# Layer norm of the query moved from GpSimd to VectorE, with all four engines' instructions reordered

## What is computed

```
x = x + xattn(ctx, layernorm(x), key_bias, seq_len)     # softmax over 128 keys, 16 heads
x = x + down(silu(gate(layernorm(x))) * up(layernorm(x)))  # inner width 512
# every linear: activation rounded to 127 / max|row|, weight to {-1, 0, 1} * mean|w|
```

## Time and profile before

| | us |
|---|---|
| median of 3 runs | 181.34 (181.11 to 182.14) |
| the profiled execution | 181.3, of which the span from first to last instruction is 179.2 |
| busy: DVE, POOL, PE, ACT | 148.7, 142.1, 141.4, 130.6 |

### The profile page before, as it was taken

The page is one execution under the profiler, slowest core; times in us unless marked ns, Lnnn a source line. Parts: engine busy times, 40 slices in busy tenths (PEclk is TensorE's granted clock), DMA queues, the critical chain, the costliest instruction groups (busy, mean ns, idle before and its releaser), DMA issues. The chain is left out here.

```text
span 179.2 us, 6662 instructions
## 1 busy us (share of the span) xinstructions
PE 141.4 (79%) x2211; PEld 89.2 (50%) x2211; DVE 148.7 (83%) x519; ACT 130.6 (73%) x197; POOL 142.1 (79%) x274
## 2 busy tenths in 40 slices
PE   0015999999998998999999995667777888988562
PEld 0013776666666665666666663112345454555441
DVE  0446767889979898988988888899999999999972
ACT  0005788988978897988888887856785989987541
POOL 7387978889867997888899999998999846774430
PEclk9999999999999999999999999555597999999985
DMA  1999993000000000000000000000001111111222
GB/s 41 308 286 299 287 294 80 4 0 5 5 4 0 5 4 2 4 4 4 0 7 4 4 2 4 2 0 2 0 15 32 46 29 46 49 44 29 60 77 59
DMA packets 16353, 9.61 MB, mean 54 GB/s; under 512 B 1088, under 2 KB 15424, under 8 KB 16320
## 3 DMA queue, kind: packets, MB, share of 16 engines
q1 hardware_dynamic: 15600, 8.39, 17.6%
q10 hardware_dynamic: 720, 0.80, 1.3%
HBM read 7.09 MB, written 2.10 MB: 51 GB/s over the span
## 5 line engine op out<-in xcount | busy, mean ns | idle before, releaser
L517 ACT ACTIVATE probs<-scores,bias_all 128x1024 f32<-128x1024 f32 x64 | 68.5, 1112 | 2.9 <-PE scores L633 2.4
L650 PE MATMUL outs<-probs,v_ones 128*32 128x128 f32 x1024 | 41.9, 283 | 0.1
L618 PE MATMUL turned<-ident_h,k_parts 128*128 128x128 f16 x128 | 19.3, 230 | 15.9 <-DVE q_parts L821 13.6
L650 PEld LDWEIGHTS outs<-probs,v_ones 128*32 128x32 f32 x1024 | 24.7, 111 | 9.0 <-issue 5.8
L633 PE MATMUL scores<-stacks 32*128 32x128 f16 x512 | 26.1, 224 | 1.4 <-DVE stacks L829 1.3
L445 POOL TENSOR_SCALAR hr<-h,h_fac 128x512 f32<-128x512 f32 x32 | 21.9, 692 | 6.5 <-DVE h_fac L910 6.2
L553 ACT ACTIVATE hqT<-turned 128x512 bf16<-128x512 int16 x32 | 19.1, 596 | 8.4 <-PE outs L719 7.7
L829 DVE COPY stacks<-turned 128x512 f32<-128x512 f32 x32 | 21.4, 670 | 4.2 <-PE turned L620 4.1
L546 ACT ACTIVATE silu_g<-scores,gate_s 128x512 f32<-128x512 f32 x32 | 22.0, 688 | 1.6 <-PE scores L691 0.6
L618 PEld LDWEIGHTS turned<-ident_h,k_parts 128*128 128x128 f16 x128 | 12.6, 102 | 19.9 <-issue 16.0
L898 DVE TENSOR_REDUCE h_peak<-h 128x1 f32<-128x512 f32 x32 | 21.5, 672 | 0.0
(11 more groups left out here) (81 smaller groups left out, 293.7 us busy)
## 6 DMA issues: line engine op xcount, KB each, us to landing
result<-x_all SPq DMA_DIRECT2D x32, 64.0 KB, 1.5
k_all<-in_ctx SPq DMA_DIRECT2D x1, 1024.0 KB, 10.8
v_all<-in_ctx SPq DMA_DIRECT2D x1, 1024.0 KB, 10.9
x_all<-in_x SPq DMA_DIRECT2D x1, 512.0 KB, 7.7
k_all<-in_ctx SPq DMA_DIRECT2D x1, 512.0 KB, 7.0
v_all<-in_ctx SPq DMA_DIRECT2D x1, 512.0 KB, 7.1
x_all<-in_x SPq DMA_DIRECT2D x2, 128.0 KB, 5.5
k_all<-in_ctx SPq DMA_DIRECT2D x2, 128.0 KB, 6.6
```

The costliest lines, as they stand in the source:

```text
L517: act.activation(probs[:, p, 8 * a:8 * a + 8, :].rearrange("p h q -> p (h q)"), scores[:, HALF * a:HALF * (a + 1)], ACT.Exp, bias=bias_all ...
L618: pe.transpose(turned_h[:, g * 128:(g + 1) * 128], k_parts[:, p4, heads, :, :].rearrange("p h c d -> p (h c d)"), ident_h[:, :])
L650: last = pe.matmul(sums_ps(p)[32 * g:32 * (g + 1), 128 * r:128 * (r + 1)], pair[:, 32 * i:32 * (i + 1)], probs[:, p, GROUPS * (2 * r + i) ...
```

## The change

- `q_norm` leaves POOL and is made by DVE with one `scalar_tensor_tensor`, `(x - mean1) * rstd1`, with `rstd1` broadcast along the features as its second tensor. `minus1_of` and its semaphore go.
- The lists of all four engines get new offsets and a new order. On DVE `q_norm` stands at -4, `q_low` at -6, `stack_out` at -7, `denom`, `attn` and `x1` at -11 (were -8, -8 and -9).
- The total of the weights moves from step 18 into `sum_a` of batch 3; clips, scales and casts of the weights move to earlier steps.
- OUT_AFTER_X goes from 14 to 12, X_BEFORE_OUT from 12 to 10. The wait of `x1_of` for `q_done` goes: both are on DVE now.

```diff
-SUM_STEP = 7
-W_TOTAL = 18
-OUT_AFTER_X = 14
-X_BEFORE_OUT = 12
+W_BATCH = 3
+OUT_AFTER_X = 12
+X_BEFORE_OUT = 10
...
# GpSimd
-            def q_norm(t, k):
-                arrived(pool, x_in, t, k)
-                pool.wait_ge(minus1_done, t.count(k))
-                pool.wait_ge(rstd1_done, t.count(k))
...
-                pool.tensor_scalar(q_f[:, t.side(k, 4), :], x_all[:, t.at(k), :].rearrange("p b d -> p (b d)"),
-                                   minus1[:, t.slot(k)], rstd1[:, t.slot(k)], ALU.add, ALU.mult).then_inc(q_done, 1)
...
-                if s == 21:
+                if s == 18:
                     w_clip(0)
-                if s == 35:
                     w_scale(0)
-                if s == 37:
+                if s == 25:
                     w_clip(1)
+                if s == 26:
                     w_clip(2)
+                if s == 30:
                     w_scale(1)
+                if s == 32:
                     w_scale(2)
-                t.run_pair(k_high, 0)
-                t.run_pair(v_beside_ones, -4)
-                t.run_pair(vare1_of, 0)
-                t.run(q_norm, -2)
-                t.run_pair(rstd1_of, 0)
-                t.run_pair(k_low, -1)
-                t.run_quad(vare2_of, -25)
+                t.run_pair(k_high, -7)
+                t.run_pair(rstd1_of, -5)
                 t.run_quad(rstd2_of, -26)
-                t.run(q_high, -2)
+                t.run(q_high, -8)
+                t.run_pair(k_low, -7)
+                t.run_pair(v_beside_ones, -10)
+                t.run_quad(vare2_of, -21)
+                t.run_pair(vare1_of, -3)
+                t.run(h_round, -56)
                 t.run(y_of, -29)
-                t.run(x_round, -39)
-                t.run(h_round, -52)
+                t.run(x_round, -46)
# ScalarE
+                if s == 23:
+                    w_cast(0)
                 if s == 37:
-                    w_cast(0)
-                if s == 38:
                     w_cast(1)
...
-                t.run(weigh_a, -5)
-                t.run(weigh_b, -5)
                 t.run(sums_of, -6)
-                t.run(xqT_out, -42)
-                t.run(silu_of, -43)
-                t.run(hqT_out, -52)
+                t.run(weigh_a, -4)
+                t.run(weigh_b, -4)
+                t.run(xqT_out, -46)
+                t.run(hqT_out, -56)
+                t.run(silu_of, -46)
# TensorE
+                if t.numbers is None and t.value(k) == W_BATCH:
+                    w_total_of(t, k)
...
+                t.run(score_b, -7)
                 t.run(stack_turn, -5)
-                t.run(score_b, -6)
-                t.run(sum_a, -7)
-                t.run(sums_turn, -8)
-                t.run(sum_b, -7)
-                t.run(score_a, -5)
+                t.run(sum_a, -8)
+                t.run(sums_turn, -9)
+                t.run(sum_b, -8)
+                t.run(score_a, -6)
+                t.run(project_gate, -45)
                 t.run(down, -55)
-                t.run(project_up, -44)
-                t.run(xq_turn, -42)
-                t.run(project_gate, -43)
-                t.run(hq_turn, -52)
+                t.run(xq_turn, -44)
+                t.run(hq_turn, -53)
+                t.run(project_up, -45)
# VectorE
+            def q_norm(t, k):
                 dve.wait_ge(mean1_done, t.count(k))
+                dve.wait_ge(rstd1_done, t.count(k))
...
+                dve.scalar_tensor_tensor(q_f[:, t.side(k, 4), :], x_all[:, t.at(k), :].rearrange("p b d -> p (b d)"),
+                                         mean1[:, t.at(k), 0:1].rearrange("p b o -> p (b o)"),
+                                         rstd1[:, t.at(k)].broadcast_to([128, D]), ALU.subtract, ALU.mult).then_inc(q_done, 1)
...
-                if s == 7:
+                if s == 8:
                     w_sum_of(0)
-                if s == 8:
                     w_sum_of(1)
-                if s == 15:
+                if s == 10:
                     w_sum_of(2)
-                if s == W_TOTAL:
+                if s == 13:
                     w_mean_of()
...
-                t.run(x1_of, -9)
                 t.run(stats1_of, 0)
-                t.run_pair(minus1_of, -1)
-                t.run(stats2_of, -9)
-                t.run(mean2_of, -11)
-                t.run(stack_out, -5)
+                t.run(q_low, -6)
                 t.run(mean1_of, 0)
-                t.run(denom_of, -8)
-                t.run_quad(minus2_of, -12)
-                t.run(q_low, -4)
-                t.run(attn_of, -8)
-                t.run(h_peak_of, -47)
-                t.run_quad(h_factor, -48)
-                t.run_quad(x_factor, -33)
-                t.run(h_of, -46)
-                t.run_quad(out_scale, -52)
-                t.run(finish, -56)
-                t.run_quad(gate_scale, -34)
-                t.run_quad(x_unit_of, -32)
-                t.run_quad(floor_of, -34)
-                t.run_quad(h_unit_of, -47)
-                t.run(y_peak_of, -31)
+                t.run(q_norm, -4)
+                t.run(denom_of, -11)
+                t.run(stats2_of, -12)
+                t.run(attn_of, -11)
+                t.run_quad(minus2_of, -18)
+                t.run(mean2_of, -14)
+                t.run(stack_out, -7)
+                t.run(x1_of, -11)
+                t.run_quad(h_factor, -49)
+                t.run(h_of, -47)
+                t.run_quad(x_factor, -30)
+                t.run_quad(out_scale, -52)
+                t.run_quad(h_unit_of, -48)
+                t.run_quad(floor_of, -33)
+                t.run(finish, -56)
+                t.run_quad(gate_scale, -30)
+                t.run_quad(x_unit_of, -29)
+                t.run(y_peak_of, -28)
+                t.run(h_peak_of, -47)
```

More of the change, by code:

```diff
@@ L174, in attention_feed_forward @@
         mean1 = sb("mean1", [128, B, 2])
-        minus1 = sb("minus1", [128, B])
         vare1 = sb("vare1", [128, B])
@@ L256, in attention_feed_forward @@
         k_hi, k_lo, v_set = sem("k_hi"), sem("k_lo"), sem("v_set")
-        stats1_done, mean1_done, minus1_done = sem("stats1_done"), sem("mean1_done"), sem("minus1_done")
+        stats1_done, mean1_done = sem("stats1_done"), sem("mean1_done")
         vare1_done, rstd1_done = sem("vare1_done"), sem("rstd1_done")
@@ L392, in rstd1_of @@
                 pool.tensor_tensor(rstd1[:, t.slot(k, 2)], vare1[:, t.slot(k, 2)], half_power[:, 0:n], ALU.pow).then_inc(rstd1_done, n)
-            def q_norm(t, k):
-                arrived(pool, x_in, t, k)
-                pool.wait_ge(minus1_done, t.count(k))
-                pool.wait_ge(rstd1_done, t.count(k))
-                if t.has(k - 4):
-                    pool.wait_ge(q_hi, t.count(k - 4))
-                    pool.wait_ge(q_lo, t.count(k - 4))
-                pool.tensor_scalar(q_f[:, t.side(k, 4), :], x_all[:, t.at(k), :].rearrange("p b d -> p (b d)"),
-                                   minus1[:, t.slot(k)], rstd1[:, t.slot(k)], ALU.add, ALU.mult).then_inc(q_done, 1)
             def q_high(t, k):
@@ L597, in w_total_of @@
                 pe.wait_ge(w_summed, 3)
-                pe.wait_ge(attn_done, t.count(k - 2))
                 pe.matmul(outs[t.side(k)][:, 0:3], ones[:, :], w_sum[:, :], start=True, stop=True).then_inc(w_total, 1)
@@ L790, in w_mean_of @@
                 dve.wait_ge(w_total, 1)
[L791 removed]
+                dve.tensor_scalar(w_mean[:, :], outs[W_BATCH % 2][:, 0:3], 1.0 / (INNER * D), QUANT_EPS, ALU.mult, ALU.max).then_inc(w_meaned, 1)
                 dve.wait_ge(w_meaned, 1)
@@ L807, in mean1_of @@
                 dve.bn_aggr(mean1[:, t.slot(k), :].rearrange("p b c -> p (b c)"), stats1[:, t.slot(k), :].rearrange("p b c -> p (b c)")).then_inc(mean1_done, 1)
-            def minus1_of(t, k):
-                n = t.group(2)
+            def q_norm(t, k):
                 dve.wait_ge(mean1_done, t.count(k))
-                dve.tensor_scalar(minus1[:, t.slot(k, 2)], mean1[:, t.slot(k, 2), 0:1].rearrange("p b o -> p (b o)"), -1.0, None,
-                                  ALU.mult).then_inc(minus1_done, n)
+                dve.wait_ge(rstd1_done, t.count(k))
+                if t.has(k - 4):
+                    dve.wait_ge(q_hi, t.count(k - 4))
+                    dve.wait_ge(q_lo, t.count(k - 4))
+                dve.scalar_tensor_tensor(q_f[:, t.side(k, 4), :], x_all[:, t.at(k), :].rearrange("p b d -> p (b d)"),
+                                         mean1[:, t.at(k), 0:1].rearrange("p b o -> p (b o)"),
+                                         rstd1[:, t.at(k)].broadcast_to([128, D]), ALU.subtract, ALU.mult).then_inc(q_done, 1)
             def q_low(t, k):
@@ L843, in x1_of @@
                 xb = x_all[:, t.at(k), :].rearrange("p b (g r i) -> p (b r) g i", g=GROUPS, r=2)
-                if not t.shift:
-                    dve.wait_ge(q_done, t.count(k))
                 dve.tensor_tensor(xb, xb, attn[:, t.side(k), :].rearrange("p (r g i) -> p r g i", r=2, g=GROUPS), ALU.add).then_inc(x1_done, 1)
```

(6 more changed lines are left out.)

3 lines of the change are left out of this document (removed).

## The result

The changed kernel takes 176.78 us (median of 4, 176.29 to 176.97) beside 181.23 us of the kernel before, run with it: a ratio of 0.9744, interval 0.9701 to 0.9786. The forecast was 178.3 us, "faster" with 0.67. The profiled execution took 176.67 us, with a span of 174.5.

A forecast was written before the change was run, and what follows sets the result against it. Attention was taken as held by order and waiting, feed-forward by DVE work. From 181.3 us, +0.3 - 1.9 - 0.45 - 0.3 - 1.1 + 0.5 = -2.95 gave 178.3 us, range 175.8 to 183.0.

The forecast's parts named there:

- the rival that TensorE sets the pace: Attention: PE fully sets 2.73 us per batch, -3.8 us instead of -1.9, total 176.4 us; chance 0.13.
- the slower rival: Attention: DVE becomes the bound at 3.0 us per batch through waits behind POOL, +3.7 us, total 183.9; chance 0.15.
- The loop: Attention: POOL's `k_high` waits for PE's key turn, which needs DVE's q_low after POOL's work; new order removes the stalls.
- The pace: Attention: spacing of ScalarE's copies of the sums, once per batch, from 2.867 to 2.80 us over 28 spacings, -1.9 us.
- 2.73 us remains their floor: Attention, PE and ACT: stack_turn moves, work is unchanged, so the best spacing of 2.73 us per batch stays the limit.
- the weights' stop: Attention: PE waits for the mean of the weights, a short stall that stays in the new order; counted in 2.80 us.
- The lock: Attention: DVE instructions with two SBUF inputs contend with POOL instructions reading SBUF, the later blocked; 0.34 us per batch allowed.
- A random moment: Attention: if DVE's instructions met POOL's at random, each would wait 0.20 us, three per batch, giving 3.0 us per batch.
- phases that miss each other: Attention: DVE and POOL mostly fall into phases without meeting, read from x1's mean of 0.300 with POOL busy 89%.
- The start: Start to second copy of the sums: first exponential 1.5 to 2 us later, mostly won back; net +0.3 (0 to +2).
- Change of stage: Attention to feed-forward: one xqT copy fewer before the table load, -0.45, and lighter POOL for the peaks of y, -0.3.
- Feed-forward and tail: Feed-forward stage and tail: -1.1 for peaks and small scales leaving the stage, +0.5 for the silu chain and later h_factor.

The follow-up runs named there:

- the four corners: Old or new order, each with `q_norm` on POOL or DVE, against the kernel before: old 1 and 0.9939, new 0.9998 and 0.9744.
- The run with the swap: Changed kernel with stack_turn put back ahead of score_b in TensorE's list: 178.30 us, ratio 0.9793, pace 2.740.
- The replaced k_low: Changed kernel with POOL's k_low subtraction replaced by a memset of zeros, leaving out the keys' fp16 remainder: 172.53 us, pace 2.591.
- The kernel with the early pair: Changed kernel with q and k work of batches 0 and 1 ahead of the stages of later loads: 173.95 us, ratio 0.9614.
- the old lists: Changed kernel with the feed-forward halves of all four engine lists and both window constants as before, attention still new: 177.35 us, ratio 0.9800.
- the runs with equal clocks: Changed kernel with stack_turn ahead of score_b (178.30 us) or batches 0 and 1 early (173.95 us), tails compared at TensorE clocks 0.90 and 0.78.

## Why the prediction was right, and where its terms were not

The sign, the mechanism and the range held; two terms were wrong by about 2.7 us each, in opposite directions, and the total is closer than its parts. That they cancel is luck. 176.78 us lies inside the stated range of 175.8 to 183.0, but under the forecast's own band of 177 to 179.7, which had 0.50; it is next to the 176.4 of the rival that TensorE sets the pace, which had 0.13. DVE became the bound of attention, as the slower rival had it, and the kernel was faster all the same.

**The loop.** "Its stalls go. What is late next is DVE." Shown: the wait before `k_high` falls from 11.2 to 1.2 us, and the four corners show that it takes the order and the lighter POOL together. POOL's saved 16.9 us alone would have bought 0.6%.

**The pace: -1.9 predicted, -4.65 measured.** The step that failed is "2.73 us remains their floor", and the 2.80 built on it. Two sizes were off. First, DVE's need: the prediction put 2.74 us per batch, the trace has 74.14 / 28 = 2.65. It is lower although x1's wait was underrated, partly because the stretch holds only 24 of 28 `q_norm` and 20 of the first statistics: the deeper offsets have moved the others into the start. Second, the floor: it lay in the place of one stage in TensorE's list, and the diff shows that this place changes. The run with the swap parts the two: with the old place 28 x (2.740 - 2.867) = -3.56 us, the move itself a further -1.1. So the larger share of the miss, 28 x 0.06 = 1.7 us, is the "friction" and the weights' stop that made 2.80 out of 2.74: the floor of 2.73 was met almost exactly as long as the stage kept its place. The sentence on PE named the move and priced it at nothing; the best spacing of a trace is a floor for that order of instructions only. "Work is unchanged" was true of the instructions and not of the time they take: the scores need 7.3 us less when their halves are neighbours. The forecast's nearness of DVE to TensorE was right all the same: 2.65 stands beside 2.58.

**The lock.** The prediction allowed 0.34 us per batch for waiting behind POOL. By the means over the whole span it is 0.50: `q_low` 523 ns where 360 is free, `q_norm` 449 for 313, x1 487 for 290. That lies between the forecast and the 0.60 of the slower rival, which had a chance of 0.15. Held against its own marks: `q_low` (under 550, right), `q_norm` (just in its band), x1 (over 450, one half of the slower rival's mark; the other half, means above 0.6, didn't come). The replaced k_low alone accounts for 0.25 us a batch. In each encounter with k_low shown the DVE instruction ends 0.08 to 0.16 us after it, a `q_norm` that is over in 0.31 when free after 1.31. The Trainium skill's rule ("SBUF — State Buffer", Who interferes with whom: the later of the two waits until the other is through) agrees with these rows in that DVE's instruction ends right behind POOL's. It isn't seen in them who was first: the two at 13.07 and 13.08 start 0.01 and 0.02 us ahead of POOL's and wait all the same. How often the two meet decided the time. "A random moment" was the wrong picture for the rival, and "phases that miss each other" for the forecast: POOL's queue waits for DVE's mean and `q_norm`, so the meetings repeat at a few fixed distances (x1 starts 0.64 to 0.66 us behind k_low six times in the 28 spacings, 0.15 to 0.20 three times), and a move by one place made the pace 0.12 us longer. One row of the prediction was misread: the `q_low` at 68.47 didn't stand behind k_low, which ended at 68.53, but behind a `q_high` of POOL that ran from 68.48 to 68.87. And one sum: 2.93 us per batch give 182.0 us, not 182.25.

**The start: +0.3 predicted, +2.90 measured.** The first exponential came at 19.45, 0.45 past the range of 18 to 19 and 2.81 us later than before, where 1.5 to 2 were counted; above all, what failed is the second half of the step, "it lost 2.1 us itself, waiting for turns 2 and 3, which the new order should have ready". From the first exponential to the second copy it takes 28.31 - 19.45 = 8.86 us, where the old order took 8.77. Four exponentials do run in a row, as foreseen, but then ScalarE waits 1.64 us for the sums (the copy at 25.21), and nothing was won back. (The terms as written, 1.5 to 2 less 2.1, would not even give +0.3, but a little under 0.) The kernel with the early pair shows that 2.6 us were the price of the deeper offsets, and of nothing that attention needs afterwards.

**Change of stage, -0.75 predicted, -1.35 measured.** One copy of xqT stands ahead of the table load, as predicted (109.83, then 110.12 above). From the last copy of the sums to the table load it takes 2.20 us for 2.64, so -0.44 where -0.45 stood; with the old lists it is 2.38. The term that was too small is the second, -0.3 for the lighter POOL: from the table load to the first h it takes 2.02 us for 2.93, -0.91, and 2.01 with the old lists. The rows show what went. Before, the first silu ended at 114.47, and h came only 0.95 us later, behind peaks of y that waited for POOL's y; after, h starts when silu ends (111.42 + 0.69 = 112.11) and is the one that waits:

```profile
113.78 0.69 ACT L546 ACTIVATE silu_g<-scores,gate_s 128x512 f32<-128x512 f32 x1
```

```profile
112.14 0.69 DVE L886 TENSOR_TENSOR h<-silu_g,scores 128x512 f32<-128x512 f32 x1 [0.53 <-ACT silu_g L537]
```

How much of this is POOL's load and how much the new order of the attention half was not run by itself; with `q_norm` on DVE in the old order the whole stretch takes 5.06 us for 5.57.

**Feed-forward and tail, -0.6 predicted, -1.4 measured.** 50.94 us from first to last h lies in the forecast's 50 to 51, but the term of -1.1 for work that leaves this stage did not come: `y_peak` stands in it 13 times for 18, and yet DVE is busy for 50.79 us where it was 50.95. `h_floor`, at 409 ns for 219, gives back 0.9 us; the rest is open. The chain of xqT, gate and silu, put at 1.6 us, takes 1.56 us (xqT at 112.00 and 113.56; the granted clock between them is 0.53, so nearly all of it at 1.2 GHz), under DVE's 50.94 / 31 = 1.64. The tail was given no gain and has -0.94 us, of which about 0.7 are the new lists, as the runs with equal clocks show above.

**"Wrong if DVE shows no idle time at all between 30 and 100 us."** It shows 0.47 us in these 70, which is next to none. This mark was set in the belief that a full DVE meant the slower rival; a full DVE at 2.70 us is faster than one at 2.87 that is idle for an eighth of its time. The other half of the mark, "or if idle time appears before h", came too, by 0.53 us at the first h and 0.15 us of idle time in the whole stage: it was no sign of a loss either, since h had come earlier.

## To carry to other kernels

A floor read as the best spacing of a trace belongs to the order of the instructions in that trace: if the diff moves a stage on that engine, the spacing may fall with the same instructions (here from 2.73 to 2.42 and 2.73 by turns), so it is a price of the order and belongs in the sum with both signs. Deeper offsets pay in the steady state and are paid once at the start; give the first batches the short distances, and both are had (here 2.8 us, more than half of what the whole change brought). Before an instruction is moved to miss another engine's, find out what releases that other one: if it is released by the same queue, the two move together, and the wait can turn up in other instructions (here `q_low` and `q_norm`).

## What was not expected of the hardware

- POOL's `tensor_scalar` over 128x128 takes 801 ns in the mean (789 at least) with subtract and the strided mean, and 473 (440 at least) with add and the packed `minus1` (529 before). Which of the two differences, the operation or the stride, makes it was not parted.
- DVE's `tensor_scalar` with one SBUF tensor and two scalars of one value per row stands behind POOL like the form with two tensors: 1.24 us beside a k_low of 1.15, 306 ns at best, 427 in the mean (449 with two tensors).
- Sixteen matmuls of 32 rows take 2 x 0.40 us when eight turns part their halves, and 0.42 or 0.72 us when the halves are neighbours.
